# Contextual attention, the paste product: one fp32 matmul becomes three fp16 ones, and work changes engines for it

## The chip, the cores and the metric

The kernel runs on one core of one Trainium2 chip. The metric is the device time of one execution in microseconds (us). Three runs of the kernel before gave 1434.99, 1431.02 and 1434.59 us, a median of 1434.59 us. The execution that was profiled took 1435.39 us, and its profile spans 1433.6 us.

## The reference

Two layers of the same function, one after the other, on 4 images of 64 channels and 80x80 pixels; the mask is zero. For one image `b`:

```
f   = b[:, :, ::2, ::2]                            # 64 x 40 x 40
w   = 3x3 patches of f                             # 1600 patches of 576 values
yi  = w . (w / max(|w|, 1e-4))^T                   # 1600 x 1600 scores
yi  = softmax(yi * 10, axis=1)                     # over the patches l
raw = 4x4 patches of b, stride 2                   # 1600 patches of 1024 values
out = sum over l of yi[l, p] * raw[l]              # "patches"
out = overlap-add of the 4x4 patches, crop, / 4    # "paste", 64 x 80 x 80
```

So an image in a layer (a unit, eight in all) is a score product, a softmax over 1600, and a paste product whose patches overlap.

## The kernel before, in words

An image of 40x40 places is cut into 14 tiles of 123 rows (`TW` = 3 strips of 41). `G` holds the 14 tiles of scores, each of 14 blocks of 123 columns. The columns are worked in four chunks, the tiles in seven pairs, so each unit has 28 slots (`SLOTS`); in one slot s every engine does its part of one tile pair in one chunk. Two units are in flight: `u` is pasted while `v` = u+1 is scored and features of `w` = u+2 are laid out. There is one body without a paste (before the first unit), seven with both, and one with a paste alone. `place(u, v, s)` turns a slot into (unit, chunk, pair).

No scheduler orders the work: each engine's function `body` is a queue written out by hand, and semaphores tie the queues together. The path of a pair towards its paste is:

- slot s+4 ahead (`LEAD`): VectorE scales and subtracts (`argument_pair`, L968), ScalarE takes two exponentials (L708), and SyncE's queue copies each result one partition down into `SH` (L326).
- `AHEAD` slots ahead: VectorE adds the shifted copy to `G` (`add_shifted`, L979), 492 columns in three chunks, 205 in the last.
- one slot ahead: VectorE adds two neighbouring tiles into `Z` (`sum_pair`, L1001; L997 and L998 for the first pair of a chunk, which also needs the strip `SHJ`). Both tiles of the pair are one instruction of 738, 984, 984 or 656 columns, by chunk.
- the slot itself: TensorE multiplies `Z` by the image blocks `B` (`paste_tile`, L521), 2 tiles x 2 halves, all fp32, and sums the 14 tiles in `psO`. In the trace one fp32 product is two MATMUL records, each with its own weight load.

Beside that runs the scoring of `v`: fp16 products into `psG` (L471), copies out of PSUM by ScalarE (L670, L683), the adds of the third row by VectorE (L883, in1 in PSUM), and the row maxima by VectorE (L898, both inputs in SBUF). Through slots 21 to 26 and 28 TensorE transposes the next image's blocks into `psM` and ScalarE copies them to `B` (L644). GpSimd has only seven small copies of `G` in a unit (`wrap`, L1109).

## Time and profile before

| | us |
|---|---|
| median of three runs | 1434.59 |
| the profiled execution | 1435.39 |
| its span | 1433.6 |
| TensorE busy | 1327.2 |
| VectorE busy | 1183.3 |
| ScalarE busy | 857.9 |
| GpSimd busy | 46.9 |
| paste products (L521) busy | 718.6 |

The busy times are unions of the records of an engine over the whole span. Engines are PE (TensorE), DVE (VectorE), ACT (ScalarE), POOL (GpSimd), and SPq (the DMA queue of SyncE). The body without a paste takes about the first 130 us, the seven full units run from there to about 1320 us, and the rest is the paste of the last unit. An engine that is busy much in the mean need not be what a given slot waits for, so the slot has to be read in order of time.

### The profile page before, as it was taken

To read this page: it belongs to the slowest core of one execution; us is meant where nothing else is said; L and a number is where in the kernel's file an instruction comes from. 1 tells how busy PE (TensorE), PEld (TensorE's weight loads), DVE (VectorE), ACT (ScalarE), POOL (GpSimd) and SP (SyncE) were. 2 spreads that over 40 slices of the span, in tenths; PEclk is the share of its full clock that TensorE was granted. 3 is DMA by queue.
4 is the path that set the end of the run, shared out by engine and by line. 5 is a ranking of instruction groups with operands and counts; after the bars stand their busy time and mean duration, and the time that the engine had idled before them with its cause. 6 is when DMAs were issued, how large, how long until landed. Compare 5 with 4: busy or idle time off the path is not lost.

```text
span 1433.6 us, 24384 instructions
## 1 busy us (share of the span) xinstructions
PE 1327.2 (93%) x7190; PEld 894.6 (62%) x7190; DVE 1183.3 (83%) x2827; ACT 857.9 (60%) x2233; POOL 46.9 (3%) x62
## 2 busy tenths in 40 slices
PE   4988999999999899999999899999999999998886
PEld 4756765676556665577656676567655766566433
DVE  3667889799888898889897888979987898978983
ACT  2677646676557565586565764666655855658331
POOL 1000000010000100001000000001000010000100
PEclk9997999999999999999999999999999999999998
DMA  5502482145822556135741359224572236313442
GB/s 91 89 1 85 109 173 76 47 116 119 163 64 67 124 113 150 49 86 127 143 117 33 104 118 179 70 52 110 126 156 67 71 107 135 94 32 96 131 136 53
DMA packets 180471, 142.54 MB, mean 99 GB/s; under 512 B 119859, under 2 KB 177267, under 8 KB 180339
## 3 DMA queue, kind: packets, MB, share of 16 engines
q1 hardware_dynamic: 180178, 140.50, 41.7%
q8 instruction: 57, 0.93, 0.3%
q10 hardware_dynamic: 160, 0.49, 0.2%
q14 instruction: 76, 0.61, 0.1%
HBM read 19.76 MB, written 13.11 MB: 23 GB/s over the span
## 4 chain that ended last, share of the span: by engine, by line
PE 54%; DVE 15%; ACT 11%; issue 8%; SPq 7%; DMA 5%; DVEq 0%; POOL 0%; ACTq 0%; POOLq 0%
PE psO L521 26%; PE psG L471 23%; SPq L326 4%; DVE G L968 4%; ACT S L697 4%; DVE Z L1001 3%; DMA SH<-G 3%; PE psG L480 3%; DVE S L898 3%; ACT G L708 2%; ACT G L683 2%; DVE G L979 2%; DMA SHJ<-G 2%; SPq L270 1%; ACT SQ L624 1%
## 5 line engine op out<-in xcount | busy, mean ns | idle before, releaser
L521 PE MATMUL psO<-Z,B 123*128 123x492 f32 (+2 forms) x1792 | 718.6, 530 | 46.0 <-DVE Z L1001 31.4
L521 PEld LDWEIGHTS psO<-Z,B 123*128 123x128 f32 x1792 | 325.8, 194 | 247.6 <-issue 133.8
L471 PE MATMUL psG<-LH,HL 128*123 128x246 f16 (+2 forms) x2616 | 407.2, 285 | 3.7 <-ACT G L670 3.0
L697 ACT ACTIVATE S<-S,nm 123x480 f32<-123x480 f32 (+3 forms) x560 | 308.5, 555 | 161.2 <-DVE nm L905 160.8
L471 PEld LDWEIGHTS psG<-LH,HL 128*123 128x123 f16 x2616 | 277.4, 137 | 125.4 <-issue 64.5
L708 ACT ACTIVATE G<-G,nb 123x492 f32<-123x492 f32 (+1 forms) x448 | 265.0, 639 | 60.3 <-DVE G L968 59.9
L898 DVE CUSTOM_DVE_ANT_0 S<-G,RB 123x492 f32<-123x492 f32 (+1 forms) x448 | 268.4, 604 | 25.8 <-ACT G L683 15.6
L979 DVE TENSOR_TENSOR G<-G,SH 123x492 f32<-123x492 f32 (+1 forms) x448 | 247.6, 591 | 48.9 <-DMA SH<-G 48.3
L968 DVE SCALAR_TENSOR_TENSOR G<-G,RA,psB 123x492 f32<-123x492 f32 (+1 forms) x448 | 270.4, 647 | 0.0
L883 DVE TENSOR_TENSOR G<-G,psG 123x492 f32<-123x492 f32 (+2 forms) x272 | 135.0, 496 | 90.4 <-PE psG L471 46.5
L1001 DVE TENSOR_TENSOR Z<-G 123x984 f32<-123x984 f32 (+2 forms) x192 | 197.2, 1028 | 0.0
L471 PE MATMUL psG<-H 128*123 128x123 f16 (+3 forms) x872 | 193.8, 284 | 0.0
L683 ACT ACTIVATE G<-psG 123x492 f32<-123x492 f32 (+3 forms) x256 | 119.7, 471 | 117.0 <-PE psG L471 76.3
L670 ACT ACTIVATE G<-psG 123x246 f32<-123x246 f32 (+1 forms) x136 | 63.6, 468 | 115.5 <-PE psG L471 115.2
L480 PEld LDWEIGHTS psG<-idn,G 123*123 123x123 f32 x672 | 95.4, 190 | 59.0 <-issue 22.4
L480 PE MATMUL psG<-idn,G 123*123 123x123 f32 x672 | 108.5, 281 | 17.9 <-ACT G L683 13.2
L471 PEld LDWEIGHTS psG<-H 128*123 128x123 f16 x872 | 102.7, 137 | 21.0 <-issue 0.4
L471 PE MATMUL psG<-HL 128*123 128x492 f16 (+2 forms) x392 | 111.8, 285 | 0.0
L697 ACT ACTIVATION_READ_ACCUMULATOR S<-S,nm 123x1 f32 x560 | 106.7, 191 | 0.0
L1109 POOL COPY G<-G 123x246 f32<-123x246 f32 x56 | 42.9, 774 | 1292.4 <-DVE mx L898 1162.5
L717 ACT ACTIVATE OSB<-psO 128x492 f32<-128x492 f32 (+2 forms) x64 | 31.4, 548 | 78.8 <-PE psO L521 78.7
L471 PE MATMUL psG<-HV 128*123 128x246 f16 (+2 forms) x240 | 67.7, 282 | 0.0
(79 smaller groups left out, 575.8 us busy)
## 6 DMA issues: line engine op xcount, KB each, us to landing
SH<-G SPq DMA_DIRECT2D x336, 214.8 KB
SH<-G SPq DMA_DIRECT2D x112, 89.2 KB
SH<-G SPq DMA_DIRECT2D x336, 19.2 KB
XP<-x SPq DMA_DIRECT2D x20, 280.0 KB, 5.7
XP<-mid SPq DMA_DIRECT2D x20, 280.0 KB, 5.5
HL<-LH SPq DMA_DIRECT2D x16, 246.5 KB, 4.5
mid<-OSB SPq DMA_DIRECT2D x48, 80.0 KB, 2.3
out<-OSB SPq DMA_DIRECT2D x48, 80.0 KB, 2.3
```

What stands on the lines that cost most here:

```text
L471: last = pe.matmul(psG[0:TW, bank, b0 * TW:b1 * TW], st[:, v % 2, p:p + TW], mv[:, v % 2, lo:lo + n], start=i == 0, stop=i == len(terms) - 1)
L480: last = pe.transpose(psG[0:TW, par, i * TW:(i + 1) * TW], G[:, c:c + TW], idn[0:TW, 0:TW])
L521: last = pe.matmul(psO[:, b, 0:n], B[:, o:o + 128], Z[:, 2 * (s % 2) + j, 0:n], start=t == 0, stop=t == TILES - 1)
L670: act.activation(to, psG[0:TW, FREE, stored * TW:w * TW], ACT.Copy).then_inc(p_copied, 1)
L683: act.activation(G[:, c:c + n], psG[0:TW, par, 0:n], ACT.Copy).then_inc(part if shared else read, 1)
L697: last = act.activation(y, y, ACT.Exp, bias=nm[:, k * TILES + t:k * TILES + t + 1], accum_out=sg[:, c:c + 1])
L708: act.activation(y, y, ACT.Exp, bias=nb[:, bass.ds(u * TILES + t, 1)]).then_inc(y_made, 1)
L883: dve.tensor_tensor((odd if par else even)[:, b0 * TW:n], rows[:, p0 * TW:p0 * TW + n - b0 * TW], psG[0:TW, par, b0 * TW:n], ALU.add).then ...
L898: dve.tensor_tensor_reduce(S[:, slot, 0:n], tile_of(j, 2 * i + par)[:, 0:n], RB[:, s0 * TW:s0 * TW + n], 1.0, 0.0, ALU.mult, ALU.max, mx[: ...
L968: dve.scalar_tensor_tensor(out=g, in0=g, scalar=RA[:, bass.ds(u * TILES + t, 1)], in1=psB[0:TW, k % 2, 0:n], op0=ALU.mult, op1=ALU.subtrac ...
L979: dve.tensor_tensor(g, g, SH[:, o % SFREE, 0:n], ALU.add).then_inc(y1_made, 1)
L1001: dve.tensor_tensor(Z[:, slot:slot + 2, 0:n], g[:, 2 * i:2 * i + 2, c0:c0 + n], g[:, 2 * i - 1:2 * i + 1, c0 - TW:c0 - TW + n], ALU.add).t ...
```

## The change

- The paste is three fp16 products in place of one fp32 one: with Z = ZH + ZL and B = BH + BL, it sums BH.ZH, BH.ZL and BL.ZH. ZL.BL is left out.
- ScalarE makes `ZH`, the fp16 copy of `Z` (`high_sums`), after the second copy of scores in its slot.
- VectorE makes `ZL` = Z - ZH (`low_sums`) at the end of its slot. `Z` is now a single buffer of one pair, and `ZH` and `ZL` are double. TensorE waits for `ZL`.
- The adds of shifted copies go from VectorE to GpSimd, three slots ahead instead of two.
- ScalarE's copies of the image blocks go to a small `B`, and GpSimd makes `BH` and `BL` from it, a copy and a subtraction of 512 columns for each of seven groups (`halve_blocks`).
- Waits that stood for "the blocks are there" on SyncE and TensorE now read `b_copied`. The mask rows of the start lie in `S`.

```diff
--- before.py
+++ after.py
@@ -42,7 +42,7 @@
 LEAD = 4
-AHEAD = 2
+AHEAD = 3
@@ -99,13 +99,18 @@
-        B = sb("B", [TW, TILES * 2 * 128], F32)
+        B = sb("B", [TW, 512], F32)
+        BH = sb("BH", [TW, TILES * 2 * 128], F16)
+        BL = sb("BL", [TW, TILES * 2 * 128], F16)
...
-        Z = sb("Z", [TW, 2 * FREE, 4 * TW], F32)
+        Z = sb("Z", [TW, FREE, 4 * TW], F32)
+        ZH = sb("ZH", [TW, 2 * FREE, 4 * TW], F16)
+        ZL = sb("ZL", [TW, 2 * FREE, 4 * TW], F16)
...
@@ -511,15 +519,16 @@  (TensorE, paste_tile)
                 if j == 0:
-                    pe.wait_ge(z_made, u * SLOTS + k * PAIRS + i + 2)
+                    pe.wait_ge(zl_made, u * SLOTS + k * PAIRS + i + 1)
                     if i == 0:
                         pe.wait_ge(o_read, (u * NK + k + 1) * 2)
                     if k == 0:
-                        pe.wait_ge(b_made, u * PAIRS + i + 1)
+                        pe.wait_ge(b_made, (u * PAIRS + i + 1) * 2)
                 for b in range(2):
                     o = (2 * t + b) * 128
-                    last = pe.matmul(psO[:, b, 0:n], B[:, o:o + 128], Z[:, 2 * (s % 2) + j, 0:n],
-                                     start=t == 0, stop=t == TILES - 1)
+                    for m, (st, mv) in enumerate(((BH, ZH), (BH, ZL), (BL, ZH))):
+                        last = pe.matmul(psO[:, b, 0:n], st[:, o:o + 128], mv[:, 2 * (s % 2) + j, 0:n],
+                                         start=t == 0 and m == 0, stop=t == TILES - 1 and m == 2)
@@ -637,11 +646,10 @@  (ScalarE, block_group)
-                if u is not None:
-                    act.wait_ge(z_used, u * SLOTS + (NK - 1) * PAIRS + g + 1 + 2)
-                    act.sem_inc(act_gate, 1)
+                act.wait_ge(b_made, (v * PAIRS + g) * 2)
+                act.sem_inc(act_gate, 1)
                 act.wait_ge(blk_psum, v * PAIRS + g + 1)
-                act.activation(B[:, g * 512:(g + 1) * 512], psM[0:TW, :], ACT.Copy).then_inc(b_made, 1)
+                act.activation(B[:, :], psM[0:TW, :], ACT.Copy).then_inc(b_copied, 1)
@@ -707,6 +715,16 @@  (ScalarE)
+            def high_sums(at, s):
+                u, k, i = at
+                n = z_cols(k)[1]
+                slot = 2 * (s % 2)
+
+                act.wait_ge(z_used, u * SLOTS + k * PAIRS + i + 1)
+                act.sem_inc(act_gate, 1)
+                act.wait_ge(z_made, u * SLOTS + k * PAIRS + i + 2)
+                act.activation(ZH[:, slot:slot + 2, 0:n], Z[:, :, 0:n], ACT.Copy).then_inc(zh_made, 1)
@@ -750,6 +769,8 @@  (ScalarE, body)
                         copy_scores(u, v, j, 1)
+                        if at_z and n == 0:
+                            high_sums(at_z, s + 1)
...
@@ -969,19 +993,9 @@  (VectorE)
-            def add_shifted(at):
...
-            def sum_pair(at, s):
+            def sum_pair(at):
...
-                dve.wait_ge(z_used, u * SLOTS + k * PAIRS + i + 1)
+                dve.wait_ge(zl_made, u * SLOTS + k * PAIRS + i)
...
-                    dve.tensor_tensor(Z[:, slot:slot + 2, 0:n], g[:, 2 * i:2 * i + 2, c0:c0 + n],
+                    dve.tensor_tensor(Z[:, :, 0:n], g[:, 2 * i:2 * i + 2, c0:c0 + n],
                                       g[:, 2 * i - 1:2 * i + 1, c0 - TW:c0 - TW + n], ALU.add).then_inc(z_made, 1)
+
+            def low_sums(at, s):
+
+                u, k, i = at
+                n = z_cols(k)[1]
+                slot = 2 * (s % 2)
+                dve.wait_ge(zh_made, u * SLOTS + k * PAIRS + i + 1)
+                dve.tensor_tensor(ZL[:, slot:slot + 2, 0:n], Z[:, :, 0:n], ZH[:, slot:slot + 2, 0:n],
+                                  ALU.subtract).then_inc(zl_made, 1)
@@ -1008,12 +1031,9 @@  (VectorE, body)
                         argument_pair(at)
-                    at_y = place(u, v, s + AHEAD)
-                    if at_y:
-                        add_shifted(at_y)
                     at_z = place(u, v, s + 1)
                     if at_z:
-                        sum_pair(at_z, s + 1)
+                        sum_pair(at_z)
@@ -1025,6 +1045,8 @@
                         for j in score_list(s):
                             score_pair(v, j)
+                    if at_z:
+                        low_sums(at_z, s + 1)
@@ -1108,8 +1130,35 @@  (GpSimd)
+            def add_shifted(at):
+                u, k, i = at
+                c0, n = p_cols(k)
+                for j, t in enumerate(arg_tiles(i)):
+                    o = k * TILES + 2 * i + j
+                    pool.wait_ge(sh_in[o % SFREE], (u * (NB // SFREE) + o // SFREE + 1) * 16 * len(SHIFT_PARTS))
+                    g = G[:, t * GLEN + c0:t * GLEN + c0 + n]
+                    pool.tensor_tensor(g, g, SH[:, o % SFREE, 0:n], ALU.add).then_inc(y1_made, 1)
+
+            def halve_blocks(u, v, g):
+
+                if u is not None:
+                    pool.wait_ge(z_used, u * SLOTS + (NK - 1) * PAIRS + g + 1 + 2)
+                    pool.sem_inc(pool_gate, 1)
+                pool.wait_ge(b_copied, v * PAIRS + g + 1)
+                high = BH[:, g * 512:(g + 1) * 512]
+                pool.tensor_copy(high, B[:, :]).then_inc(b_made, 1)
+                pool.wait_ge(b_made, (v * PAIRS + g) * 2 + 1)
+                pool.tensor_tensor(BL[:, g * 512:(g + 1) * 512], B[:, :], high, ALU.subtract).then_inc(b_made, 1)
+
             def body(u, v):
                 for s in BODY:
+                    at = place(u, v, s + AHEAD)
+                    if at:
+                        add_shifted(at)
+                    if v is not None and (NK - 1) * PAIRS <= s < SLOTS - 1:
+                        halve_blocks(u, v, s - (NK - 1) * PAIRS)
+                    if v is not None and s == SLOTS:
+                        halve_blocks(u, v, PAIRS - 1)
```

VectorE's queue, one slot in which a pair of the third chunk is summed, before. The names are those above; an `ISA` row is the product and maximum of L898 (`S,mx<-G,RB`) or the reading of its result (`mx`):

```order
 L968 SCALAR_TENSOR_TENSOR G<-G,RA,psB 123x492 x2
 L979 TENSOR_TENSOR G<-G,SH 123x492 x2
 L1001 TENSOR_TENSOR Z<-G 123x984
 L883 TENSOR_TENSOR G<-G,psG 123x492
 L898 ISA S,mx<-G,RB 123x492
 L898 ISA mx 123x1
 L905 TENSOR_SCALAR nm<-mx 123x2
 L883 TENSOR_TENSOR G<-G,psG 123x492
 L898 ISA S,mx<-G,RB 123x492
 L898 ISA mx 123x1
```

and the same slot now:

```order
 L992 SCALAR_TENSOR_TENSOR G<-G,RA,psB 123x492 x2
 L1015 TENSOR_TENSOR Z<-G 123x984
 L907 TENSOR_TENSOR G<-G,psG 123x492
 L922 ISA S,mx<-G,RB 123x492
 L922 ISA mx 123x1
 L929 TENSOR_SCALAR nm<-mx 123x2
 L907 TENSOR_TENSOR G<-G,psG 123x492
 L922 ISA S,mx<-G,RB 123x492
 L922 ISA mx 123x1
 L1024 TENSOR_TENSOR ZL<-Z,ZH 123x984
```

Two adds of 492 columns have left the front of the slot, and one subtraction of 984 columns stands at its end, behind the maxima.

GpSimd's queue, before, was per unit these copies (`wrap`):

```order
 L1109 COPY G<-G 123x2x123 [waits max_made,z_made,y1_made]
 L1109 COPY G<-G 123x2x123 [waits y1_made] x6
```

and now, at the slots in which blocks are halved:

```order
 L1140 TENSOR_TENSOR G<-G,SH 123x205 [waits sh_in3]
 L1140 TENSOR_TENSOR G<-G,SH 123x205 [waits sh_in0]
 L1140 TENSOR_TENSOR G<-G,SH 123x205 [waits sh_in1]
 L1149 CAST BH<-B 123x512 [waits z_used,b_copied]
 L1151 TENSOR_TENSOR BL<-B,BH 123x512 [waits b_made]
 L1140 TENSOR_TENSOR G<-G,SH 123x205 [waits sh_in2]
```

GpSimd has two adds in every slot, each waiting for the landing of its shifted copy, and two more instructions in seven of the 28 slots.

## Rows read from the trace of the kernel before

**Rows 1.** The page, part 1: engine, busy us (share of the span), instructions.
```profile
PE 1327.2 (93%) x7190; PEld 894.6 (62%) x7190; DVE 1183.3 (83%) x2827; ACT 857.9 (60%) x2233; POOL 46.9 (3%) x62
...
```

**Rows 2.** Busy time by stretch: bounds, length, busy us (instructions), granted clock, DMA.
```profile
645.00:814.00 169.00, 161.44 (x897) 108.97 (x896) 146.88 (x351) 107.44 (x282) 5.34 (x7) 1.00 0.45 105
...
1320.00:1433.60 113.60, 88.92 (x227) 43.98 (x226) 80.54 (x137) 34.70 (x67) 5.14 (x7) 0.93 0.38 105
```

**Rows 3.** Order of time on VectorE, one slot: start, us, engine, line, operation.
```profile
727.63 1.36 DVE L968 SCALAR_TENSOR_TENSOR G<-G,RA,psB 123x492 f32<-123x492 f32 x2
728.91 1.25 DVE L979 TENSOR_TENSOR G<-G,SH 123x492 f32<-123x492 f32 x2
730.07 1.18 DVE L1001 TENSOR_TENSOR Z<-G 123x984 f32<-123x984 f32 x1
731.16 0.66 DVE L883 TENSOR_TENSOR G<-G,psG 123x492 f32<-123x492 f32 x1
731.74 0.67 DVE L898 CUSTOM_DVE_ANT_0 S<-G,RB 123x492 f32<-123x492 f32 x1
...
732.45 0.17 DVE L905 TENSOR_SCALAR nm<-mx 123x2 f32<-123x2 f32 x1
732.57 0.67 DVE L883 TENSOR_TENSOR G<-G,psG 123x492 f32<-123x492 f32 x1
...
733.74 1.36 DVE L968 SCALAR_TENSOR_TENSOR G<-G,RA,psB 123x492 f32<-123x492 f32 x2
```

**Rows 4.** Order of time on TensorE: fp16 products, and fp32 paste products.
```profile
726.25 1.41 PE L471 MATMUL psG<-LH,HL 128*123 128x492 f16 x6
...
1394.48 6.87 PE L521 MATMUL psO<-Z,B 123*128 123x492 f32 x16 [0.98 <-DVE Z L1001]
```

**Rows 5.** The page, part 5: busy us, mean ns of one, idle before, releaser.
```profile
L521 PE MATMUL psO<-Z,B 123*128 123x492 f32 (+2 forms) x1792 | 718.6, 530 | 46.0 <-DVE Z L1001 31.4
...
L979 DVE TENSOR_TENSOR G<-G,SH 123x492 f32<-123x492 f32 (+1 forms) x448 | 247.6, 591 | 48.9 <-DMA SH<-G 48.3
...
L883 DVE TENSOR_TENSOR G<-G,psG 123x492 f32<-123x492 f32 (+2 forms) x272 | 135.0, 496 | 90.4 <-PE psG L471 46.5
L1001 DVE TENSOR_TENSOR Z<-G 123x984 f32<-123x984 f32 (+2 forms) x192 | 197.2, 1028 | 0.0
```

**Rows 6.** Groups by line and shape on ScalarE: copies out of PSUM.
```profile
L670 ACT ACTIVATE G<-psG 123x492 f32<-123x492 f32 x64 | 36.9, 576 | 45.5 <-PE psG L471 45.4
...
L670 ACT ACTIVATE G<-psG 123x246 f32<-123x246 f32 x72 | 26.8, 372 | 70.1 <-PE psG L471 69.8
```

**Rows 7.** Order of time on GpSimd: two memsets, and copies at two places.
```profile
0.73 2.97 POOL L1091 MEMSET XP<- 128x3444 f32 x1 [0.29 <-POOLq L1131]
3.64 0.92 POOL L1092 MEMSET SQ<- 128x984 f32 x1
...
645.31 0.73 POOL L1109 COPY G<-G 123x246 f32<-123x246 f32 x2 [147.97 <-DVE mx L898]
...
655.89 0.92 POOL L1109 COPY G<-G 123x246 f32<-123x246 f32 x1 [2.83 <-DVE G L979]
```

**Rows 8.** Order of time on VectorE beside those copies of GpSimd.
```profile
645.07 1.35 DVE L968 SCALAR_TENSOR_TENSOR G<-G,RA,psB 123x492 f32<-123x492 f32 x2
...
655.64 0.92 DVE L1001 TENSOR_TENSOR Z<-G 123x738 f32<-123x738 f32 x1
656.48 0.41 DVE L883 TENSOR_TENSOR G<-G,psG 123x246 f32<-123x246 f32 x1
```

**Rows 9.** Order of time on VectorE, a slot of the last stretch (no scores).
```profile
1351.67 1.36 DVE L968 SCALAR_TENSOR_TENSOR G<-G,RA,psB 123x492 f32<-123x492 f32 x2
...
1354.11 1.18 DVE L1001 TENSOR_TENSOR Z<-G 123x984 f32<-123x984 f32 x1
1355.20 1.35 DVE L968 SCALAR_TENSOR_TENSOR G<-G,RA,psB 123x492 f32<-123x492 f32 x2
```

**Rows 10.** Order of time on ScalarE: the two exponentials of a slot.
```profile
729.25 1.30 ACT L708 ACTIVATE G<-G,nb 123x492 f32<-123x492 f32 x2
```

More of the change, by code:

```diff
@@ L738, in body @@
                     at = place(u, v, s + LEAD)
+                    at_z = place(u, v, s + 1)
                     pairs = score_list(s) if v is not None else []
@@ L760, in body @@
                         softmax_pair(at)
+                    if at_z and not pairs:
+                        high_sums(at_z, s + 1)
                     if s == SLOTS and v is not None:
@@ L805, in _ @@
         def _(dve):
[L806 removed]
+            dve.memset(Z[0:MROWS, 0:LAYERS, :], 0.0)
+            dve.memset(S[0:MROWS, 0, :], 0.0).then_inc(mask_step, 1)
             dve.memset(halves[:, :], 0.0).then_inc(halves_cleared, 1)
```

26 lines of the change are left out of this document (10 added, 16 removed).

## The prediction

> **What bounds the kernel now.** I read the busy times first: TensorE is busy 93% of the span and VectorE 83% [rows 1]. That looks like a kernel bound by TensorE, so I cut it by stretch. In a full unit of 169.0 us TensorE is busy 161.4 and VectorE 146.9 [rows 2]. Neither is free, and the mean can't say which one a slot waits for. The order of time can. In a slot of the third chunk VectorE goes from one `argument_pair` to the next in 6.11 us (727.63 to 733.74) without a gap: arguments 1.28, shifted adds 1.16, the sum 1.09, then the adds of the third row and the maxima [rows 3]. TensorE's part of the same slot is two pairs of fp32 paste products and some 16 fp16 products: 8 records at 0.42 us are 3.4 us, and 16 at 0.21 are 3.3 [rows 4], together 6.7 less what overlaps. So the two engines run side by side, and in the slots of the long chunks VectorE sets the period. To make TensorE faster helps only as far as VectorE gets no slower. Therefore the sum has to be made on VectorE.
>
> **TensorE.** The fp32 paste runs at (6.87 - 0.58) / 15 = 0.42 us from start to start of a record (16 records, the last one taken as 0.58 long), 0.84 for a product of 492 columns; fp16 products of 492 columns follow each other at (1.41 - 0.37) / 5 = 0.21 us, 0.37 being the length of one [rows 4]. Three of them are 0.62. Both go by columns, so 26% of 718.6 us [rows 5] is saved at most, 185 us in all or 23 per unit. The weights are 128 columns in place of 123, which I cost at nothing, since loads lie beside products. If TensorE alone were the bound this would end near 1250 us.
>
> **VectorE, per unit (an eighth of the sums in the page).**
> - Shifted adds go: 247.6 / 8 = 31.0 us off. Their waits for the landing of `SH` go too, 48.9 / 8 = 6.1 [rows 5].
> - `low_sums` come: 28 of them, with the columns of the sums and two inputs in SBUF like those: 197.2 / 192 = 1.03 us each [rows 5], 28.8 us on. The fp16 operand could make it cheaper, down to half; it could hardly be dearer. I take the full price, since one input is still fp32.
> - So the change of owner gives back as much as it takes: -31.0 - 6.1 + 28.8 = -8.3 us per unit. The slot of rows 3 goes from 6.11 to 6.11 - 1.16 + 1.09 = 6.04.
>
> **ScalarE.** A copy costs 0.372 us at 246 columns and 0.576 at 492 [rows 6], 0.83 ns per column, so `ZH` of 984 columns is 0.99 us and of 738 or 656 0.78 and 0.71. That is 24 us more per unit, where ScalarE has over 60 us idle [rows 2]. Beside the scores it is hidden: it starts when the sum and the second score copy are done, while VectorE still has 2 us of third rows and maxima. In the last stretch there are no scores between sum and difference, and VectorE waits for it (below).
>
> **GpSimd, and what it does to VectorE.** The trace has no addition on GpSimd. A memset gives its rate, (2.97 - 0.92) / 2460 = 0.83 ns per column, and two copies of 246 columns take 0.73, so 0.36 each, 0.16 over the rate [rows 7]. From below, an add of 492 columns at that rate is 0.57 us; if two reads and a write follow one another it is 1.39. I take two passes, 0.82 + 0.16 = 1.0 us, in the middle and because both operands have to be read. A unit has 42 such, 14 of 205 columns at 0.5, and seven halvings at 0.6 + 1.0: 42 + 7 + 11 = 60 us of 169. GpSimd has time for it, and with three slots' lead (18 us) against an exponential, a transfer and an add the sums are not late.
>
> The point is the port. The copy of GpSimd that starts at 645.31 runs beside an operation of VectorE that has one input in PSUM, and costs 0.36. The one issued at 655.89 lies under a sum with both inputs in SBUF (655.64 to about 656.48, when the next operation starts) and takes 0.92: it ends 0.33 after 656.48, as if it had begun when the sum was over [rows 7, 8]. So on this chip GpSimd is kept out while VectorE reads two operands from SBUF. The trace shows that in one direction only, because GpSimd never began first. I take it to hold the other way too: an operation of VectorE with two SBUF inputs waits until a running GpSimd operation is over.
>
> The Trainium skill (SBUF — State Buffer, Who interferes with whom) says just that: an operation of VectorE with two SBUF inputs and one of GpSimd that reads SBUF lock each other out for a whole instruction, and whichever comes first holds the port. By that rule the direction not shown here holds; the measured direction agrees with it, 0.92 against 0.36 us.
>
> What it costs: in the slot of rows 3, as changed, the operations with two SBUF inputs are the sum 1.09, two maxima of 0.6 and the difference 1.09, 3.4 of 6.04 us. Between them lie open stretches of 1.28 (arguments), 0.58 (third row), 0.8 (read, negation, third row) and 0.1. An add of 1.0 us that comes up at an even chance anywhere in the slot begins at once in an open stretch, or at the start of the next one, and VectorE's next closed operation waits for what is left: 0.39 on average in the arguments (weight 0.21), 0.42 from under the sum (0.18), 0.71 in the third row (0.10), 0.2 and 0.9 from under the two maxima (0.10 each), 0.60 in the 0.8 (0.13), 0 from under the difference (0.18); together 0.43 us. For 42 adds 18.1 us, for the short ones 14 x 0.1, for the halvings 7 x 0.58: 23.6 us per unit. Of that some falls where VectorE waits anyway. In the unit of rows 2 it idles 169.0 - 146.9 = 22.1 us, of which 6.1 were the landings already taken off; of the other 16, mostly third rows that wait for TensorE (L883 in [rows 5]), I let a little under half take it up, 7.3. Net per unit: -8.3 + 23.6 - 7.3 = +8.0, and for seven units +56.
>
> GPSIMD Engine Reference of the Trainium skill (3.1, Elementwise) gives an add of 2048 fp32 columns as 4497 ns, about twice VectorE's; as an estimate 492 columns are then 1.1 to 1.2 us, which no row here shows. By it the delays would be about 28 us per unit and the sum some 30 us higher.
>
> **The last stretch.** A slot there is 3.53 us on VectorE (1351.67 to 1355.20), with nothing behind the sum [rows 9]. Now: arguments 1.28, sum 1.09, the wait for `ZH` 0.99, the difference 1.09: 4.45. ScalarE's two exponentials (1.30 [rows 10]) begin after the first argument and are over about when the sum is. So +0.92 for 14 slots, +0.46 for the seven of the first chunk (0.78 + 0.84 - 1.16) and up to 0.9 for the last seven: 22 us. Against it stand about 8 us of landings no longer waited for in order and 4 of TensorE's shorter end: +10. GpSimd's adds fall into the wait for `ZH`, which is open. The first stretch, without a paste, I leave as it is.
>
> **Sum.** The profiled execution took 1435.39 us (0.8 above the median). 1435.4 + 56 + 10 = 1501, less 0.8 is 1500 us.
>
> **Rivals.**
> - *The port does not work backwards* (GpSimd yields, or its operations fall under other waits). Then -8.3 per unit, and some 3 more, since a faster TensorE shortens the 90.4 us that third rows waited [rows 5]: -11.3 x 7 + 10 gives 1366. For it: VectorE's records in the trace never show a stretched operation, which shows nothing as no GpSimd operation came first. Against it: the copies behave like a whole-instruction lock, to 0.03 us. Chance 0.24.
> - *The lock is there, but landings come in step with the slot.* A shifted copy lands a fixed time after its argument, so the two adds have fixed places. At the best place the two cost 0.42 together in place of 0.86: 11.8 us per unit, -8.3 + 11.8 - 7.3 = -3.8, so 1435 - 27 + 10 = 1418. Chance 0.13.
> - *GpSimd is dearer.* At 1.39 us an add fits in no open stretch and costs 0.75 on average: 41 us per unit, +25 net, 1435 + 178 + 10 = 1620. The port would be asked for 84 us by VectorE and about 80 by GpSimd, as much as the unit is long. It needs adds above some 1.2 us to decide. Chance 0.13.
> - *The paste is not faster:* if weight loads of 128 fp16 columns stopped the array, 3 products would cost 0.84 and nothing is won on TensorE; with the lock the time is as forecast, since VectorE sets it. Inside my range, no case of its own.
>
> **Numbers.** My forecast 0.47 (1440 to 1560), 0.24 the port free, 0.13 in step, 0.13 dearer, 0.03 for something else, faster. In step has its own spread across the old time: 0.08 of it faster, 0.03 within 0.3%, 0.02 slower; of the 0.03, 0.02 and 0.01. Faster: 0.24 + 0.08 + 0.02 = 0.34; within 0.3% (4 us, about what a measurement of this kernel can tell from no change) 0.04; slower 0.47 + 0.13 + 0.02 = 0.62. The range for 8 in 10 is 1370 to 1580; that of the likeliest alone 1440 to 1560.
>
> **What would show it.** Right: on VectorE, L1015, L1024 and L922 with means well above those of the same shapes before (1.03 and 0.60), in a fraction of their instances, each ending with an add of GpSimd; adds of 492 columns with a mean near 1.4, of which 0.4 under VectorE; TensorE's busy time down by over 100 us and its waits for L1024 long; slots of 6.5 to 7.5 us. In the last stretch a gap of about 1 us before each L1024. Wrong: if L1015 and L1024 keep 1.03 us everywhere while GpSimd's adds overlap them, the lock works one way and the first rival holds. If GpSimd's adds take under 0.7 us, the size of the delay is wrong; if VectorE waits for ScalarE's `ZH` in the middle slots, I have hidden what isn't hidden.

## The result, and the profile after

The changed kernel takes 1644.41 us (median of four runs, 1635.08 to 1647.25) against 1432.80 for the kernel before on the same chip: 1.1477 times as long, 95% interval 1.1432 to 1.1522. The forecast was 1500 with a range to 1580. The direction and the lock on the port were right. The size was not: +212 us where +65 was forecast, because the lock cost more than I had priced and idle time gave back less. The profiled execution took 1645.91 us, its span is 1643.9.

Part 1 of the page after, in the columns of [rows 1]:

```profile
PE 1276.1 (78%) x8086; PEld 863.1 (53%) x8086; DVE 1428.2 (87%) x2604; ACT 1054.8 (64%) x2457; POOL 767.4 (47%) x622
```

TensorE is busy 51 us less than before, VectorE 245 us more. The chain of work that ended last has changed hands. Before it read "PE 54%; DVE 15%", now:

```profile
DVE 39%; PE 23%; issue 15%; ACT 11%; SPq 6%; DMA 4%; POOL 1%; DVEq 1%; ACTq 0%; POOLq 0%
```

By stretch (bounds, length, busy us and instructions of PE, PEld, DVE, ACT, POOL, then granted clock, DMA share, GB/s) the body without a paste, the seven full units and the tail are:

```profile
0.00:142.00 142.00, 99.28 (x722) 80.54 (x723) 91.62 (x266) 85.50 (x238) 28.91 (x28) 0.95 0.34 63
142.00:1514.00 1372.00, 1100.72 (x7042) 747.98 (x7040) 1246.93 (x2235) 914.66 (x2138) 672.28 (x540) 0.91 0.38 89
1514.00:1643.90 129.90, 76.14 (x327) 34.60 (x325) 89.68 (x105) 54.63 (x81) 66.24 (x56) 0.86 0.32 89
```

A full unit lasts 1372/7 = 196 us against 169 [rows 2], with VectorE busy 178 of it against 147. Counted from the first sum of one unit to the first of the next, 185 of the 210 us lie in the seven full units, 26 in the tail (118 us before, 144 now), and the start is 1 us shorter. Counted by the first paste product of each unit it is 7 us in the start, 184 in the units and 19 in the tail. The difference is the way of a unit's first pair: its first product came 1.0 to 2.5 us after its first sum (128.9 and 130.0 at the first unit), and now comes 9 us after it (127.8 and 137.1), since maxima and the difference stand between.

The groups by line and shape on VectorE (busy us, mean ns of one, idle before, releaser):

```profile
L922 DVE CUSTOM_DVE_ANT_0 S<-G,RB 123x492 f32<-123x492 f32 x336 | 282.9, 847 | 18.0 <-ACT G L691 13.4 <-issue 2.3 <-ACT S L705 0.4
L992 DVE SCALAR_TENSOR_TENSOR G<-G,RA,psB 123x492 f32<-123x492 f32 x336 | 226.9, 717 | 0.0
L1024 DVE TENSOR_TENSOR ZL<-Z,ZH 123x984 f16<-123x984 f32 x112 | 175.4, 1566 | 24.8 <-ACT ZH L726 24.2
L1015 DVE TENSOR_TENSOR Z<-G 123x984 f32<-123x984 f32 x96 | 129.4, 1348 | 21.8 <-POOL G L1140 21.8
L929 DVE TENSOR_SCALAR nm<-mx 123x2 f32<-123x2 f32 x224 | 85.3, 381 | 7.7
L907 DVE TENSOR_TENSOR G<-G,psG 123x492 f32<-123x492 f32 x128 | 85.0, 664 | 27.4 <-PE psG L479 26.3 <-ACT G L678 0.8
```

The operations sort cleanly. The maxima (0.67 in [rows 3]), the sum (1.18 there) and the new difference have both inputs in SBUF, and their means are 0.85, 1.35 and 1.57 us. The third rows (L907) and the arguments (L992) have an input in PSUM and stay at 0.66 and 0.72. The surprise is L929, the negation of two columns with one input: 0.17 us in [rows 3], now 0.38 on average and 1.20 at the longest.

On GpSimd the adds of 492 columns and the halvings:

```profile
L1140 POOL TENSOR_TENSOR G<-G,SH 123x492 f32<-123x492 f32 x336 | 511.4, 1538 | 444.6 <-DMA SH<-G 444.1
...
L1151 POOL TENSOR_TENSOR BL<-B,BH 123x512 f16<-123x512 f32 x56 | 81.5, 1456 | 4.5
L1149 POOL CAST BH<-B 123x512 f16<-123x512 f32 x56 | 43.2, 772 | 266.8 <-ACT B L652 266.6
```

Two stretches in order of time show that each engine can lock the other out. In the tail GpSimd has this:

```profile
1547.56 2.63 POOL L1140 TENSOR_TENSOR G<-G,SH 123x492 f32<-123x492 f32 x2 [3.23 <-DMA SH<-G]
1552.20 1.22 POOL L1140 TENSOR_TENSOR G<-G,SH 123x492 f32<-123x492 f32 x1 [2.01 <-DMA SH<-G]
1553.60 1.95 POOL L1140 TENSOR_TENSOR G<-G,SH 123x492 f32<-123x492 f32 x1 [0.18 <-DMA SH<-G]
```

and VectorE:

```profile
1546.70 1.18 DVE L1024 TENSOR_TENSOR ZL<-Z,ZH 123x984 f16<-123x984 f32 x1 [1.09 <-ACT ZH L726]
...
1549.07 2.16 DVE L1015 TENSOR_TENSOR Z<-G 123x984 f32<-123x984 f32 x1
1552.32 2.13 DVE L1024 TENSOR_TENSOR ZL<-Z,ZH 123x984 f16<-123x984 f32 x1 [1.09 <-ACT ZH L726]
1554.38 1.35 DVE L992 SCALAR_TENSOR_TENSOR G<-G,RA,psB 123x492 f32<-123x492 f32 x2
```

An add of 492 columns takes 1.22 us when nothing stands in its way (1552.20). The difference issued 0.12 behind it, at 1552.32, takes 2.13 instead of 1.18, and ends 1.03 after the add's end at 1553.42: it began when the add was over. The next add, issued at 1553.60, waits for that difference in turn and takes 1.95. Whoever comes second waits for the whole rest of the first.

In a slot with scores VectorE looks like this:

```profile
845.71 1.07 DVE L929 TENSOR_SCALAR nm<-mx 123x2 f32<-123x2 f32 x1
846.68 0.66 DVE L922 CUSTOM_DVE_ANT_0 S<-G,RB 123x492 f32<-123x492 f32 x1
847.27 0.08 DVE L922 DVE_READ_ACCUMULATOR2_ANT mx<- 123x1 f32 x1
847.27 2.19 DVE L1024 TENSOR_TENSOR ZL<-Z,ZH 123x984 f16<-123x984 f32 x1
```

beside two adds on GpSimd

```profile
845.38 3.04 POOL L1140 TENSOR_TENSOR G<-G,SH 123x492 f32<-123x492 f32 x2 [5.40 <-DMA SH<-G]
```

The negation waits 0.9 us for the first add, the difference 1.0 for the second. TensorE waits for that difference, and its clock falls. Products of the paste ahead of the wait and behind it, and then the busy time in the wait and in the 4 us after it (columns as above):

```profile
844.80 0.37 PE L530 MATMUL psO<-ZH,BH 123*128 123x492 f16 x1
845.00 0.37 PE L530 MATMUL psO<-ZL,BH 123*128 123x492 f16 x1
...
849.52 0.38 PE L530 MATMUL psO<-ZH,BH 123*128 123x492 f16 x1 [1.98 <-DVE ZL L1024]
...
850.37 0.62 PE L530 MATMUL psO<-ZH,BH 123*128 123x492 f16 x1
850.78 0.62 PE L530 MATMUL psO<-ZL,BH 123*128 123x492 f16 x1
```

```profile
846.00:849.50 3.50, 0.70 (x5) 0.50 (x4) 3.50 (x5) 2.73 (x7) 2.35 (x2) 1.00 0.03 9
849.50:853.50 4.00, 3.98 (x13) 2.21 (x14) 3.17 (x8) 1.65 (x4) 0.55 (x1) 0.57 0.19 51
```

In the 3.5 us of the first window TensorE is busy 0.70. Then the granted clock of the next 4 us is 0.57, mostly the lower level of 1.2 GHz, and products of 492 columns follow each other at 0.41 us instead of 0.21.

### The profile page after: what moved, and what is told of

Same layout as the page of the kernel before. It is cut to its first block, busy times and chain, and to the rows that moved or that the text cites. A ratio compares the mean times of both kernels' runs of the same rounds, so it can differ in the third digit from the quotient of the medians.

```text
span 1643.9 us, 27019 instructions
## 1 busy us (share of the span) xinstructions
PE 1276.1 (78%) x8086; PEld 863.1 (53%) x8086; DVE 1428.2 (87%) x2604; ACT 1054.8 (64%) x2457; POOL 767.4 (47%) x622
## 4 chain that ended last, share of the span: by engine, by line
DVE 39%; PE 23%; issue 15%; ACT 11%; SPq 6%; DMA 4%; POOL 1%; DVEq 1%; ACTq 0%; POOLq 0%
PE psG L479 10%; PE psO L530 10%; DVE S L922 10%; DVE ZL L1024 9%; DVE G L992 6%; DVE Z L1015 6%; ACT S L705 4%; DMA SH<-G 3%; DVE G L907 3%; SPq L334 2%; PE psG L488 2%; ACT ZH L726 2%; SPq L278 2%; ACT G L716 2%; SPq L322 1%
## 5 line engine op out<-in xcount | busy, mean ns | idle before, releaser
L1140 POOL TENSOR_TENSOR G<-G,SH 123x492 f32<-123x492 f32 (+1 forms) x448 | 613.6, 1384 | 592.6 <-DMA SH<-G 592.1
L530 PE MATMUL psO<-ZH,BH 123*128 123x492 f16 (+2 forms) x896 | 340.7, 380 | 269.6 <-DVE ZL L1024 261.9
L922 DVE CUSTOM_DVE_ANT_0 S<-G,RB 123x492 f32<-123x492 f32 (+1 forms) x448 | 349.6, 784 | 20.4 <-ACT G L691 13.4
L530 PE MATMUL psO<-ZL,BH 123*128 123x492 f16 (+2 forms) x896 | 338.5, 378 | 0.0
L530 PE MATMUL psO<-ZH,BL 123*128 123x492 f16 (+2 forms) x896 | 337.4, 377 | 0.0
L479 PEld LDWEIGHTS psG<-LH,HL 128*123 128x123 f16 x2616 | 284.6, 141 | 88.7 <-DVE G L907 11.8
L1024 DVE TENSOR_TENSOR ZL<-Z,ZH 123x984 f16<-123x984 f32 (+2 forms) x224 | 290.9, 1299 | 41.5 <-ACT ZH L726 40.9
L530 PEld LDWEIGHTS psO<-ZH,BH 123*128 123x128 f16 x896 | 94.4, 105 | 373.3 <-DVE ZL L1024 308.6
L992 DVE SCALAR_TENSOR_TENSOR G<-G,RA,psB 123x492 f32<-123x492 f32 (+1 forms) x448 | 269.4, 643 | 0.0
L1015 DVE TENSOR_TENSOR Z<-G 123x984 f32<-123x984 f32 (+2 forms) x192 | 229.5, 1195 | 23.8 <-POOL G L1140 23.8
L726 ACT ACTIVATE ZH<-Z 123x984 f16<-123x984 f32 (+2 forms) x224 | 201.9, 901 | 65.6 <-DVE Z L1015 51.8
L907 DVE TENSOR_TENSOR G<-G,psG 123x492 f32<-123x492 f32 (+2 forms) x272 | 134.0, 493 | 64.3 <-PE psG L479 33.1
L530 PEld LDWEIGHTS psO<-ZH,BL 123*128 123x128 f16 x896 | 95.6, 107 | 91.5 <-issue 28.7
L530 PEld LDWEIGHTS psO<-ZL,BH 123*128 123x128 f16 x896 | 95.1, 106 | 63.2 <-issue 18.5
```

The lines of the kernel that those rows point to most:

```text
L479: last = pe.matmul(psG[0:TW, bank, b0 * TW:b1 * TW], st[:, v % 2, p:p + TW], mv[:, v % 2, lo:lo + n], start=i == 0, stop=i == len(terms) - 1)
L530: last = pe.matmul(psO[:, b, 0:n], st[:, o:o + 128], mv[:, 2 * (s % 2) + j, 0:n], start=t == 0 and m == 0, stop=t == TILES - 1 and m == 2)
L726: act.activation(ZH[:, slot:slot + 2, 0:n], Z[:, :, 0:n], ACT.Copy).then_inc(zh_made, 1)
L907: dve.tensor_tensor((odd if par else even)[:, b0 * TW:n], rows[:, p0 * TW:p0 * TW + n - b0 * TW], psG[0:TW, par, b0 * TW:n], ALU.add).then ...
L922: dve.tensor_tensor_reduce(S[:, slot, 0:n], tile_of(j, 2 * i + par)[:, 0:n], RB[:, s0 * TW:s0 * TW + n], 1.0, 0.0, ALU.mult, ALU.max, mx[: ...
L992: dve.scalar_tensor_tensor(out=g, in0=g, scalar=RA[:, bass.ds(u * TILES + t, 1)], in1=psB[0:TW, k % 2, 0:n], op0=ALU.mult, op1=ALU.subtrac ...
```

## The experiments

Ratios are to the kernel before, run on the same chip; the interval is 95%. Where two changed kernels are compared in us, they can come from different chips, on which the kernel before took 1429 to 1433 us.

### The adds back on VectorE

```diff
 (VectorE, body; GpSimd keeps the halvings; AHEAD = 2)
+                    at_y = place(u, v, s + AHEAD)
+                    if at_y:
+                        add_shifted(at_y)
```

> The changed kernel with the adds of shifted copies back on VectorE, two slots ahead; GpSimd keeps the wraps and the halvings. Theory (port: VectorE's operations with two SBUF inputs wait for GpSimd's): the stretching goes except beside the halvings, but 29 us of adds per unit come back in its place, so about as slow as the changed kernel: 1600 to 1640 us, with L1024 of 984 columns at 1.18 us mean (1.57 there) and the negation at 0.17 (0.38). Rival 1 (the longer chain sum, high half, low half, paste is what costs, the adds on GpSimd are free): VectorE gets 31 us more per unit on top, 1850 us. Rival 2 (the adds come too late from GpSimd): under 1550.

Measured: 1627.71 us, 1.1378 (1.1361 to 1.1395). VectorE is busy 1452.9 us, 89% of the span; maxima of 492 columns take 680 ns, sums of 984 1174 and differences of 984 1179. So 31 us of adds a unit, moved away from the engine that sets the time, brought nothing: the kernel is 17 us faster with them than without (14 by the ratios, whose intervals don't overlap). The lock costs at least what the adds cost. The negation is at 195 ns, near its 0.17, so the halvings alone hardly touch it.

### The adds on GpSimd, alone

```diff
-AHEAD = 2
+AHEAD = 3
 (VectorE, add_shifted)
-                    dve.tensor_tensor(g, g, SH[:, o % SFREE, 0:n], ALU.add)
 (GpSimd, add_shifted; the paste stays fp32)
+                    pool.tensor_tensor(g, g, SH[:, o % SFREE, 0:n], ALU.add).then_inc(y1_made, 1)
```

> The kernel before (fp32 paste) with one thing of the change: the adds of shifted copies on GpSimd, three slots ahead. Port theory: VectorE loses 31 us of adds and 6 of waits per unit and gets 20 to 25 back as stretched sums, maxima and negations, so 1380 to 1440 us, with the sums of 984 columns near 1.35 us and TensorE busy over 95%. Rival 1 (adds on GpSimd are free): TensorE's 161 us per unit become the bound, 1380, and no operation of VectorE is longer than before. Rival 2 (late adds): above 1500, with waits of the sums for GpSimd.

Measured: 1438.40 us, 1.0051 (1.0032 to 1.0071), within the window but no gain, and TensorE is busy 92%, not over 95. Of the 247.6 us of adds that left VectorE, 172 came back: it is busy 1107.3 instead of 1183.3.

```profile
L898 DVE CUSTOM_DVE_ANT_0 S<-G,RB 123x492 f32<-123x492 f32 x336 | 261.5, 784 | 24.4 <-ACT G L683 18.9 <-issue 1.5
...
L992 DVE TENSOR_TENSOR Z<-G 123x984 f32<-123x984 f32 x96 | 133.1, 1387 | 49.4 <-POOL G L1106 43.9 <-PE psO L521 5.3
```

The other 76 went into idle time. Once a unit VectorE's sum waits for GpSimd. In order of time on VectorE, then on GpSimd:

```profile
887.75 2.07 DVE L992 TENSOR_TENSOR Z<-G 123x984 f32<-123x984 f32 x1 [6.83 <-POOL G L1106]
```

```profile
886.38 6.14 POOL L1106 TENSOR_TENSOR G<-G,SH 123x492 f32<-123x492 f32 x4 [14.06 <-DMA SH<-G]
```

and in SyncE's queue:

```profile
872.08 6.58 SPq L270 DMA_DIRECT2D XP<-mid  x6
878.77 6.39 SPq L326 DMA_DIRECT2D SH<-G  x8
```

The shifted copies stand behind six image loads, which take 6.58 us to issue. GpSimd sits 14 us without one, then makes four adds in a row, and VectorE's sum, issued after 6.83 us of waiting, takes 2.07. Of the 48.9 us of waits for landings that I had taken off nothing is gained: the sums now wait 54.7 us for GpSimd.

### GpSimd writes for as long as it would add

```diff
-                    pool.tensor_tensor(g, g, SH[:, o % SFREE, 0:n], ALU.add)
+                    pool.memset(IDLE[:, 0:1345 if k < NK - 1 else 624], 0.0)
```

> The changed kernel, but in place of each add GpSimd writes zeros for the same time (1345 or 624 columns, 1.22 or 0.62 us) to a tile that nobody reads; shifted copies aren't added and the low halves of the blocks aren't used (BH stands three times... twice with ZH, once with ZL). Same instruction counts on all engines. Port theory in its narrow form (what is shared is the reading side): sums, differences and maxima are back at 1.18, 1.18 and 0.67 us; only the negation (one input, both ends in SBUF) may stay stretched. Then the time is what I had worked out without the lock, some 8 us less per unit than before and a longer tail: 1370 to 1430. Rival (GpSimd blocks VectorE whatever it does): as slow as the changed kernel, 1600 or more, with the same stretched operations.

Measured: 1497.58 us, 1.0482 (1.0448 to 1.0516). In place of the adds GpSimd is occupied for the same time but reads nothing from SBUF (the halvings still read; the kernel leaves out the adds and the blocks' low halves):

```profile
L923 DVE CUSTOM_DVE_ANT_0 S<-G,RB 123x492 f32<-123x492 f32 x336 | 231.7, 695 | 17.6 <-ACT G L692 11.4 <-issue 2.3 <-ACT S L706 0.4
...
L1025 DVE TENSOR_TENSOR ZL<-Z,ZH 123x984 f16<-123x984 f32 x112 | 132.1, 1179 | 19.5 <-ACT ZH L727 18.6
L1016 DVE TENSOR_TENSOR Z<-G 123x984 f32<-123x984 f32 x96 | 112.8, 1175 | 42.1 <-POOL IDLE L1142 42.1
...
L930 DVE TENSOR_SCALAR nm<-mx 123x2 f32<-123x2 f32 x224 | 68.5, 306 | 7.7
...
L1142 POOL MEMSET IDLE<- 123x1345 f32 x336 | 410.1, 1221 | 454.3 <-DMA SH<-G 447.5
```

and one negation in order of time, then the two memsets beside it:

```profile
867.70 1.03 DVE L930 TENSOR_SCALAR nm<-mx 123x2 f32<-123x2 f32 x1
```

```profile
867.48 2.50 POOL L1142 MEMSET IDLE<- 123x1345 f32 x2 [6.95 <-DMA SH<-G]
```

Sum and difference are plain again, while a memset as long as an add runs. It is GpSimd's reading that locks two-input operations out. Against the changed kernel this run is 147 us shorter, with 203 us less of VectorE's busy time. The negation stays at 306 ns, so GpSimd's writing holds it up too: the one shown ends at 868.73, just after the first memset (867.48 + 1.22 = 868.70), and 58 of the 72 stretched ones end within 0.04 us after a memset in this way, the other 14 after a halving. The time itself missed its window. By my terms VectorE's busy time is 1183.3 - 247.6 + 230.2 = 1166 and its idle 250.3 - 48.9 = 201; they are 1225 and 268. The idle is in the waits for `IDLE` (the place of the adds, 44.8 us in 8 waits), for `ZH` (40.7) and for `SHJ` (31.8).

The Trainium skill (SBUF — State Buffer, Who interferes with whom) says that a GpSimd instruction that only writes does not contend with two SBUF inputs, and that `tensor_scalar`, where its operands meet certain conditions, can enter a two-port mode that does contend with it. The trace agrees with both, with 1179 ns for the difference and 306 for the negation. My sum had only the operations with two SBUF inputs in it.

### The adds back, and no low half of the sums

```diff
-                    for m, (st, mv) in enumerate(((BH, ZH), (BH, ZL), (BL, ZH))):
+                    for m, (st, mv) in enumerate(((BH, ZH), (BL, ZH), (BL, ZH))):
...
-                    if at_z:
-                        low_sums(at_z, s + 1)
```

> As e1_adds_back, and without the low halves of the sums: no L1024, and the third product is BL with ZH again (ZL is left out). VectorE has the work of the kernel before, TensorE the fp16 paste, ScalarE the high halves. It asks what the faster paste is worth alone. Theory (VectorE sets the period): TensorE's busy time falls by 150 us or more, the time by only 1 to 4%: 1375 to 1420 us. Rival (TensorE was the bound, as its 93% said): 1433 less 23 us per unit, under 1300.

Measured: 1454.46 us, 1.0163 (1.0138 to 1.0187), above the window. Against the run with the adds back this removes 224 differences and 173 us, with TensorE's waits for them: `low_sums` is the dearest part of the change. But what is left should have beaten the kernel before, since TensorE is busy 1217.3 us in place of 1327.2, and it doesn't. VectorE does the work of before in 1219.7 us in place of 1183.3.

### And no halvings on GpSimd

```diff
-                act.activation(B[:, :], psM[0:TW, :], ACT.Copy).then_inc(b_copied, 1)
+                act.activation(BH[:, g * 512:(g + 1) * 512], psM[0:TW, :], ACT.Copy).then_inc(b_copied, 1)
 (GpSimd, body, twice)
-                        halve_blocks(u, v, s - (NK - 1) * PAIRS)
```

> e4_no_low_half (1454 us) without the halvings on GpSimd: ScalarE writes the blocks as fp16 at once, and the three products are all BH with ZH (both low halves are left out and the output is a multiple). GpSimd has only the wraps, as in the kernel before. Theory (the halvings stretch VectorE, whose busy time in e4 was 37 us above the kernel before for the same work): VectorE's busy time is back at 1183 and the time at 1400 to 1425. Rival (the detour over ScalarE's ZH is what eats the faster paste): still 1445 or more, with VectorE idle longer.

Measured: 1419.89 us, 0.9920 (0.9899 to 0.9940). So the 112 instructions of the halvings, 128 us of GpSimd's time, cost 35 us, and VectorE's busy time falls by 39 to 1180.3. (The pair also differs in what ScalarE's copy of a block waits for; I did not separate that.) And a paste of three fp16 products in place of one fp32, with no new work on VectorE and none on GpSimd, is worth 11 us.

### One fp16 product

```diff
-        B = sb("B", [TW, TILES * 2 * 128], F32)
+        B = sb("B", [TW, TILES * 2 * 128], F16)
-        Z = sb("Z", [TW, 2 * FREE, 4 * TW], F32)
+        Z = sb("Z", [TW, 2 * FREE, 4 * TW], F16)
```

> The kernel before with Z and B written as fp16 by the instructions that made them in fp32, and one fp16 product in place of the fp32 one (both low halves are left out). VectorE, ScalarE and GpSimd have the work of before, TensorE some 67 us less per unit. Theory (VectorE sets the period once TensorE yields): the time goes only to VectorE's busy time and the waits that aren't TensorE's, 1300 to 1370, and not to 1433 - 8 x 67. Rival (TensorE's clock falls when it idles, which gives the saving back): above 1400 with a granted clock under 0.93.

Measured: 1387.97 us, 0.9693 (0.9668 to 0.9719).

```profile
PE 994.1 (72%) x6294; PEld 722.7 (52%) x6294; DVE 1179.7 (85%) x2827; ACT 855.2 (62%) x2233; POOL 46.9 (3%) x62
```

TensorE gives up 333 us of busy time and the kernel gets 43 us faster. With the queues as they are this is about all that a faster paste can bring; the time is above the window that I gave. VectorE's chain of arguments, adds and sums stands: 47% of the chain that ended last is VectorE's, 8% TensorE's. The granted clock fell to 0.848, as the rival said, but the time stayed under the rival's 1400. How much of the saving the clock took back no run separates.

### The negation on ScalarE, the rest as changed

```diff
-                    negate(v, j - 1)
+                    act.activation(nm[:, c:c + 2], mx[:, 2 * (j % 2):2 * (j % 2) + 2], ACT.Copy, scale=-1.0)
```

> The changed kernel with 26 of 28 negations per unit (L929, two columns, 0.17 us alone and 0.38 in the mean) made by ScalarE. Port theory: a small operation of VectorE pays the whole wait for GpSimd; take it away and part of its 47 us of stretching goes, the rest meets the next operation with two inputs: 10 to 40 us less, 1605 to 1635. Rival (the stretching of the negation is a wait in the shadow of others): no change, 1640 to 1650; ScalarE gets some 45 us more work and could also make it slower.

Measured: 1610.67 us, 1.1248 (1.1217 to 1.1280), 34 us below the changed kernel. 208 operations of 0.17 us, 35 us in all, are gone and VectorE's busy time falls by 69: the other half was their waiting for the port. Not all of the waiting goes: the maxima of 492 columns rise from 847 to 865 ns.

### The adds held to open places

```diff
+                    if now:
+                        pool.wait_ge(*((zl_made, now), (z_made, now + 2))[j])
+                        pool.sem_inc(pool_gate, 1)
```

The first add of a slot waits until the last difference is made, so that it falls under the arguments; the second until the sum is made, so that it falls under a third row.

> The changed kernel with GpSimd's two adds of a slot gated: the first may begin only when the difference of the slot before is done (so beside the arguments, 1.28 us in which VectorE reads one operand from SBUF), the second when the sum is done (beside the third row, 0.58 of its 1.22 us). Same instructions otherwise. Port theory: per slot VectorE is stretched by 1.22 - 0.58 = 0.64 us at most in place of the 1.16 measured, so 12 us less per unit: 1540 to 1600 us, differences at 1.18 us again, the maxima still long. Rival (stretching doesn't depend on the place): 1640 or more, as gates only delay the adds.

Measured: 1603.07 us, 1.1202 (1.1179 to 1.1224), 41 us off, 3 short of the window. The difference is nearly plain, but the maxima, the negation and the sums (1338 ns at 984 columns) are not:

```profile
L922 DVE CUSTOM_DVE_ANT_0 S<-G,RB 123x492 f32<-123x492 f32 x336 | 274.6, 823 | 14.5 <-ACT G L691 13.4 <-ACT S L705 0.4 <-issue 0.4
...
L1024 DVE TENSOR_TENSOR ZL<-Z,ZH 123x984 f16<-123x984 f32 x112 | 134.7, 1203 | 15.7 <-ACT ZH L726 15.6
...
L929 DVE TENSOR_SCALAR nm<-mx 123x2 f32<-123x2 f32 x224 | 93.4, 417 | 7.7
```

The first add takes 1.22 us and starts some 0.26 after the two arguments (570.79 against 570.53 in one slot), which take 1.28, so its end sticks out over the sum: 75 of 96 long sums are stretched, 60 of them by under 0.1 us. The second does not fit under a third row of 0.6, and what sticks out falls on the maximum or the negation.

### Each add in quarters

```diff
+                    for a in range(0, n, TW):
+                        b = min(a + TW, n)
+                        g = G[:, t * GLEN + c0 + a:t * GLEN + c0 + b]
+                        last = pool.tensor_tensor(g, g, SH[:, o % SFREE, a:b], ALU.add)
```

> The changed kernel with each add on GpSimd cut into instructions of 123 columns (four for 492, two for 205). If the port is held for a whole instruction, a short instruction holds it for 0.26 + 0.17 = about 0.42 us, and VectorE gets in between: the longest stretches fall from 1.2 to about 0.45 us and VectorE's busy time by 60 to 130, the time to 1540 to 1610, though GpSimd's own work grows by some 0.4 us per add. Rival (GpSimd keeps the port from one instruction to the next when it has work queued): stretches stay at 1.2 us or grow, time 1640 or more.

Measured: 1562.58 us, 1.0931 (1.0911 to 1.0952), 82 us below the changed kernel although GpSimd is busy 1157.6 us instead of 767.4.

```profile
L1142 POOL TENSOR_TENSOR G<-G,SH 123x123 f32<-123x123 f32 x1456 | 929.1, 672 | 193.6 <-DMA SH<-G 193.3
```

A quarter takes 0.44 us when nothing stands in its way, 672 ns on average here. VectorE is busy 1313.7 instead of 1428.2. More of its operations are stretched, but each by less: 109 of 336 maxima of 492 columns by over 0.1 us, by 0.27 on average, where it was 90 by 0.68, and 94 of 112 differences of 984 by 0.23, where it was 44 by 1.0. VectorE gets in between two quarters even while GpSimd has work queued. In the tail, from 1479 to 1500, GpSimd's quarters follow each other without an idle moment, and a difference beside them is only 0.3 us longer than its 1.18:

```profile
1479.37 20.82 POOL L1142 TENSOR_TENSOR G<-G,SH 123x123 f32<-123x123 f32 x33 [0.69 <-DMA SH<-G]
```

```profile
1487.05 1.47 DVE L1024 TENSOR_TENSOR ZL<-Z,ZH 123x984 f16<-123x984 f32 x1 [1.09 <-ACT ZH L726]
```

So what one operation of VectorE waits for is the rest of one instruction of GpSimd, not of its queue. The price is GpSimd's own time: it now makes up 27% of the chain that ended last. It is the fastest complete form of the three-product kernel that I ran.

### The adds on GpSimd beside one fp16 product

```diff
 (to the kernel with one fp16 product; AHEAD = 3; VectorE, add_shifted)
-                    dve.tensor_tensor(g, g, SH[:, o % SFREE, 0:n], ALU.add)
 (GpSimd)
+                    pool.tensor_tensor(g, g, SH[:, o % SFREE, 0:n], ALU.add).then_inc(y1_made, 1)
```

> e6_one_fp16_product (1388 us, VectorE the bound, TensorE with room) with the adds of shifted copies on GpSimd, three slots ahead. In e2 the same move left the time where it was (1438), and there TensorE was busy 92%. Port theory: VectorE's busy time falls by some 76 us as in e2 (248 off, 172 of stretching back), and now that shows: 1320 to 1360 us. Rival (the stretching always eats the move): 1380 to 1400.

Measured: 1391.54 us, 0.9733 (0.9710 to 0.9756): no gain over one product alone, even where VectorE has no new work, and in the rival's window. Its busy time falls by 71 us, its idle time grows by 76:

```profile
DVE Z L992 <- POOL G L1106: 75.3, 20, 8.6
DVE Z L988 <- DMA SHJ<-G: 69.2, 28, 6.1
```

(us in all, times, longest.) Each unit has one wait of some 8 us, after the image loads, as in the run with the adds alone.

### The same with the adds held to open places

```diff
+                    if j == 0:
+                        pool.wait_ge(add_gate, slot)
+                    elif now:
+                        pool.wait_ge(z_made, now + 2)
```

> e7_one_product_pool_adds with GpSimd's first add of a slot gated to the start of VectorE's arguments and the second to the end of the sum. In e9 gates took 41 us from the changed kernel. Port theory: 10 to 40 us less than e7. Rival (the gates delay the adds until the sums wait for them, since there is less slack in shorter slots): no gain or slower than e7.

Measured: 1412.70 us, 0.9882 (0.9865 to 0.9899): 21 us slower, where I expected a gain. The rival, that held adds make the sums wait, is not what happened: VectorE's idle time stays (277.2 and 275.5 us), and its waits for GpSimd fall from 75.3 to 69.4. Its busy time rises from 1108.9 to 1135.7, nearly all of it in the maxima (338.9 to 375.0): 109 of 336 of the long ones are stretched in place of 72. A second add that begins when the sum is done sticks out over the third row onto the maximum: beside 55 of those 109 runs an add that began within 0.25 us of a sum's end, beside 1 of the 72 without gates. So these gates put adds where they hurt more than by chance.

### One product and the negation on ScalarE

```diff
 (to the kernel with one fp16 product; adds stay on VectorE)
-                    negate(v, j - 1)
+                    act.activation(nm[:, c:c + 2], mx[:, 2 * (j % 2):2 * (j % 2) + 2], ACT.Copy, scale=-1.0)
```

> e6_one_fp16_product (1388 us; adds on VectorE, nothing new on GpSimd) with 26 of 28 negations per unit on ScalarE, which waits for them anyway and has over 500 us idle. Theory (VectorE sets the period in e6): its busy time falls by 35 us and the time by 15 to 40, to 1345 to 1375. Rival (the chain maximum, negation, exponential, next maximum gets longer by ScalarE's 0.2 us and a semaphore and holds VectorE up): 1385 or more.

Measured: 1363.24 us, 0.9520 (0.9503 to 0.9536), the fastest of all, 68 us below the kernel before on its chip. It leaves out both low halves. GpSimd has only its seven copies, VectorE is busy 1134.3 us. Against one product alone VectorE's busy time is 45 us lower and the kernel 25 us faster, with next to no lock in play.

## Why the prediction was wrong in size

Two terms of the sum failed: the stretch that the lock causes (23.6 us per unit, measured 32.8), and what idle time was to give back (13.4, measured 4.3). Divide the profiled executions by eight units. The measured values are the pages' totals (VectorE idle is span less busy, 250.3 before and 215.7 after).

| us per unit | forecast | measured |
|---|---|---|
| adds leave VectorE | -31.0 | -31.0 |
| `low_sums` at plain length | +28.8 | +28.8 |
| VectorE stretched by GpSimd | +23.6 | +32.8 |
| VectorE idle (landings 6.1, taken up 7.3) | -13.4 | -4.3 |
| net | +8.0 | +26.3 |

The third line measured is the busy time's +30.6 less the first two. Eight times 26.3 is the 210 us. The forecast was for the seven full units, with the tail by itself. Counted in those alone, between first sums, the third line is 34.2, the fourth -5.6 and the net 26.4.

**The lock works backwards**: right, and the question on which most hung. Rival one (the port free in that direction, 1366) is refuted by the difference at 1552.32 in the tail and by the memset run, which takes the reading away and returns every two-input operation to its plain length.

**The size of the stretch** is the first step that failed, a third too low, for two reasons. An add of 492 columns was taken at 1.0 us between bounds of 0.57 and 1.39; it takes 1.22, and the halvings' subtraction of 512 columns 1.15 alone. I had written that the dearer rival "needs adds above some 1.2 us to decide", and that is where it was: its 1620 us was closer than my 1500, though not by its own sum: its 41 us per unit are about as much too high as my 23.6 are too low, and the idle time, which both had wrong, made up for it. And my list of what the port can stop held two-input operations only. By the pages' means the stretching is (784 - 604) x 448 = 81 us in the maxima (604 ns before), 61 in the differences against the 1.028 of [rows 5], 32 in the sums, 47 in the negation (381 against 169), together 221 of 262; the rest is spread over small operations, such as a difference of 40 columns once a unit that takes 1.12 us. The negation alone is 5.9 us of the 9.2 per unit that I missed. The add's length is the lesser part, as far as I can tell: put into my even-chance sum, 1.22 us makes 0.61 per add in place of 0.43 and some 31 us per unit, an estimate, while 26.9 were measured without the negation. With it on ScalarE VectorE is relieved of 69 us, 34 more than its plain length.

**What idle time takes up** is the second, and as large: 9.1 us per unit (7.8 in the full units alone). I assumed that delays fall partly where VectorE waits anyway, and that the waits for landings go with the adds. The groups say what happened. The waits of L883, about half of them for TensorE and half for ScalarE [rows 5], went from 90.4 to 64.3, 3.3 per unit where I took 7.3. The waits for landings, 48.9, became 23.8 for GpSimd: 3.1 instead of 6.1, since the sum needs the same landing whoever adds it. And new waits for `ZH` came, 41.5:

```profile
L1024 DVE TENSOR_TENSOR ZL<-Z,ZH 123x984 f16<-123x984 f32 (+2 forms) x224 | 290.9, 1299 | 41.5 <-ACT ZH L726 40.9
```

24.5 of them are in the tail, where a wait is 0.81 to 1.09 us by its columns, near the forecast (0.71 to 0.99), but the rest lies in slots with scores, which I had called hidden. One of them, ScalarE first, then VectorE:

```profile
852.67 0.58 ACT L691 ACTIVATE G<-psG 123x492 f32<-123x492 f32 x1 [1.93 <-PE psG L488]
853.15 1.01 ACT L726 ACTIVATE ZH<-Z 123x984 f16<-123x984 f32 x1
```

```profile
854.20 1.18 DVE L1024 TENSOR_TENSOR ZL<-Z,ZH 123x984 f16<-123x984 f32 x1 [1.39 <-ACT ZH L726]
```

`ZH` stands behind a copy of scores, and that one waited 1.93 us for TensorE, which ran mostly at the lower clock level from 849.5 to 853.5. The late difference had come back as a late copy.

**TensorE**: the step to 0.21 us per fp16 product is right where it runs at full clock (844.80, 845.00). The saving of up to 185 us in busy time (over 100 was one of my signs of being right) came out as 51 (26% of 718.6 is 187, not 185, which changes nothing). Slots with a late `ZL` leave it waiting (261.9 us in 127 waits), and after the wait shown (849.52) the products ran at the lower clock level; the mean granted clock fell from 0.983 to 0.911. No run isolates what the clock costs. That it doesn't decide is likely: TensorE's share of the chain that ended last fell from 54% to 23%, and with one product the clock is lower still, 0.848, and the kernel is faster.

**The owner's exchange** (-8.3 per unit without the lock) is not shown by any run. The nearest, the memset run, is 67 us slower than before, though its two-input operations are plain. 35 us are the price of the halvings by the pair of runs that differ in them. The stretched negation is another 31 us of busy time. How much of the latter is already in the former I did not separate.

**The tail** was +26 against +10, counted from the first sum of the last unit. VectorE's idle time there grew by 8 us (33 to 41), close to the forecast, with 25.1 of waits for `ZH` and fewer for landings. Its busy time grew by 18.5 (84.7 to 103.2), for which I had put nothing: adds did not all fall into the wait for `ZH`, as at 1549.07, where the sum takes 2.16. The start, which I had left as it was, did not grow.

Rival two (in step, 1418): its 11.8 us per unit are 28 slots at 0.42 and leave out the halvings. It did not come about, since the adds have no fixed place in the slot; 90 of 336 maxima, 44 of 112 differences and 22 of 96 sums of the long shapes are stretched, by 0.1 to 1.1 us. Rival three is treated above.

What stays open: how the memset run's 67 us divide, and how the idle time that the forecast took back would have come out without the lock. A version of the three-product kernel that combines quarters and the negation on ScalarE was not run.

## What to carry to other kernels

Moving work from VectorE to GpSimd is not removing it: price each moved instruction at its own length on GpSimd against VectorE's two-input operations and its small single-input ones, and take nothing back from "idle time" without naming the wait that absorbs it. If it has to be moved, short instructions are worth a try: four per add took 82 of the 212 us back here. And before making TensorE faster at a price elsewhere, run it with the price left out: one fp16 product showed a ceiling of 43 us for the whole paste, against 173 us that the low halves of the sums alone cost.
